# A two-layer graph attention kernel: VectorE ends layer 0's last chunk, x's product and layer 1's weights change place, and some steps change engine

## The reference

```python
# layer 0: x [4096,64], E [4096,64], adj [4096,4096] int32 (mostly 0)
scores = (x @ W @ a1)[:, None] + (E @ W @ a2)[None, :]
e = where(scores > 0, scores, 0.2 * scores); e = where(adj > 0, e, NEG_BIG)
x = layernorm(x + elu(softmax(e, axis=1) @ E + x))
# layer 1: the new x is on both sides
wh = x @ W1
e = leaky_relu((wh @ a_src)[:, None] + (wh @ a_dst)[None, :], 0.01)
x = layernorm(x + softmax(where(adj > 0, e, NEG_INF), axis=1) @ wh + bias)
```

## Time and profile before

| | |
|---|---|
| median of 3 runs | 646.89 us (645.05 to 647.01) |
| the profiled execution | 648.09 us, its span 646.3 us |
| busy: DVE, ACT, PE, POOL | 554.9, 535.4, 509.3, 178.7 us |
| granted PE clock, mean | 0.96 |
| DMA | 76.16 MB, most of it in the first half |

### The profile page before, as it was taken

One profiled execution on the slowest core, in us unless ns is written; L12 is line 12 of the kernel. 1 busy time (PEld: TensorE's weight loads), 2 busy tenths in 40 slices (PEclk: granted clock), 3 DMA queues, 4 the chain that ended last, 5 costly groups with the idle time before them and its releaser, 6 DMA issues.

```text
span 646.3 us, 14279 instructions
## 1 busy us (share of the span) xinstructions
PE 509.3 (79%) x6039; PEld 237.3 (37%) x6039; DVE 554.9 (86%) x758; ACT 535.4 (83%) x618; POOL 178.7 (28%) x116
## 2 busy tenths in 40 slices
PE   1307777889989799989987875578887988899994
PEld 1204444333443334434454532233333333333352
DVE  2899997999799998989669688877979998889795
ACT  0969993989999997899989687648997999689783
POOL 2241000266027830465001056005200340121050
PEclk9999787999999999999999898879999999989998
DMA  9998994766568636630100100000001000000000
GB/s 219 363 369 297 351 335 138 263 222 238 216 208 283 245 126 260 211 111 1 50 3 2 35 2 2 34 0 2 10 2 32 2 17 1 18 2 17 1 14 14
DMA packets 18252, 76.16 MB, mean 118 GB/s; under 512 B 6300, under 2 KB 8524, under 8 KB 9996
## 3 DMA queue, kind: packets, MB, share of 16 engines
q1 hardware_dynamic: 17304, 74.87, 33.0%
q0 software_dynamic: 112, 0.28, 0.2%
q10 hardware_dynamic: 772, 0.10, 0.1%
HBM read 74.16 MB, written 1.09 MB: 116 GB/s over the span
## 4 chain that ended last, share of the span: by engine, by line
issue 31%; DVE 25%; ACT 21%; PE 16%; POOL 5%; DMA 1%; ACTq 1%; POOLq 0%; DVEq 0%
ACT Pm L783 17%; DVE junk L903 11%; PE acc L1169 8%; DVE zps L1051 7%; PE zps L1224 5%; ACT zps L775 2%; DVE v L880 2%; PE acc L1176 1%; DMA acol<-in_L_gnn_weight_a 1%; POOL tAB L542 1%; POOL rstd L587 1%; DVE D L923 1%; POOL tAB L545 1%; DVE tot L965 0%; POOL o L526 0%
## 5 line engine op out<-in xcount | busy, mean ns | idle before, releaser
L783 ACT ACTIVATE Pm<-zps,ebias 128x1024 f32<-128x1024 f32 (+1 forms) x320 | 292.0, 934 | 60.3 <-DVE zps L1051 47.9
L1224 PE MATMUL zps<-D,v 128*128 128x128 bf16 x2048 | 166.8, 225 | 59.9 <-DVE D L923 32.6
L775 ACT ACTIVATE zps<-S_row,ntau_col 128x1024 f32<-128x1024 f32 (+1 forms) x203 | 195.1, 964 | 5.3
L1224 PEld LDWEIGHTS zps<-D,v 128*128 128x128 fp8e4 x2048 | 120.2, 100 | 201.5 <-ACT zps L775 89.6
L1169 PE MATMUL acc<-Pm,VE 128*32 128x512 f32 (+2 forms) x1280 | 148.8, 539 | 19.8 <-ACT Pm L783 13.7
L1051 DVE SCALAR_TENSOR_TENSOR zps<-S_row,tau_col,zps 128x1024 f32<-128x1024 f32 (+1 forms) x117 | 118.5, 1034 | 50.7 <-PE zps L1224 50.4
L1169 PE MATMUL acc<-Pm,X 128*32 128x512 f32 (+2 forms) x1280 | 141.8, 532 | 21.5 <-ACT Pm L783 20.1
L903 DVE CUSTOM_DVE_ANT_0 junk<-v,adj_in 128x2048 int8<-128x2048 int8 (+3 forms) x80 | 154.5, 1954 | 1.7 <-ACT adj_in L664 1.7
L903 DVE CUSTOM_DVE_ANT_0 junk<-v,u_row 128x2048 int8<-128x2048 int8 x64 | 152.4, 2397 | 0.2
L1176 PE MATMUL acc<-Pm,ones 128*32 128x256 f32 (+1 forms) x1280 | 87.8, 348 | 0.0
L518 POOL TENSOR_TENSOR tAB<-flag,totW 128x520 f32<-128x520 f32 (+1 forms) x8 | 10.9, 1366 | 260.3 <-issue 166.1
(11 more groups left out here) (163 smaller groups left out, 261.5 us busy)
## 6 DMA issues: line engine op xcount, KB each, us to landing
adj_in<-in_adj SPq DMA_DIRECT2D x62, 1024.0 KB, 5.5
S_row<-S_rows_scratch SPq DMA_DIRECT2D x6, 512.0 KB, 4.0
Pm<-in_adj SPq DMA_DIRECT2D x2, 1024.0 KB, 5.6
...
```

The lines of the kernel that those rows point to most:

```text
L775: a.activation(mask_of(n), S_row[:, C % 2, 0:R(C) * P], ACT.Relu, bias=ntau_col[:, layer(C), n % JT:n % JT + 1]).then_inc(seed_done, 1)
L783: a.activation(Pm_of(k, 0, R(C) * P), mask_of(k), ACT.Exp, bias=ebias[:, layer(C), int(seeded(k)), J:J + 1])\
L1224: last = t.matmul(mask[:, r * P:(r + 1) * P], v[:, chunks[C][1] + r, J * P:(J + 1) * P], D[:, C % 2, PART * second + r, :], start=(r * P % ...
```

## The change

It does five things.

1. `BY_VECTOR` takes in chunk 4, layer 0's last: its `add_up`, `normalise` and `scale` run on DVE within chunk 5, and POOL keeps the power. `IN_FIRST` moves these up (scores from step 19 to 13, the transposes of the rows from 22 to 18), `THIRD` lists the steps of the maxima over chunk 6's second stretch of columns, and the second `D` comes at step 22 and no longer at 25, with its weights apart (`weights_of_parts`, step 24).
2. x's product runs on DVE, just ahead of its sum, and no longer on POOL.
3. W0 goes first on SP's queue, ahead of E; a0, W1 and a1 stay on ACT's. The semaphore `w_loaded` is one for each layer, and the setup turns and spreads layer 0's weights alone. Layer 1's are repeated, turned and saved between chunk 0's row maxima, in PSUM of `acc`.
4. ACT does a Tanh on one column (`warm`) ahead of the first `convert`.
5. `SEEDS`: chunk 3 has 23 seeded steps and no longer 26, chunks 6 and 7 have 18 each and no longer 20.

```diff
-SEEDS = ((29, 28, 28, 26, 24), (20, 20, 20, 10, 0))
+SEEDS = ((29, 28, 28, 23, 24), (20, 18, 18, 10, 0))
-    IN_FIRST = dict(reciprocal=6, elu=8, sums=10, squares=14, scores=19, rows=22, maxima=23, second=25)
+    IN_FIRST = dict(add_up=5, elu=8, normalise=9, scores=13, rows=18, maxima=20, second=22, weights=24)
+    THIRD = (1, 3, 7, 11, 15, 16, 18, 23)
-    BY_VECTOR = (NC - 2, LAST)
+    BY_VECTOR = (NC - 2, NC - 1, LAST)
...
             if C == NC:
                 n = R(nxt)
-                return [(nxt, r, 1) for r in range(n) if 1 + r * 20 // n == J] + \
+                return [(nxt, r, 1) for r in range(n) if THIRD[r] == J] + \
                        [(NC, r, 3) for r in range(R(NC)) if at("maxima", C) + r // 2 == J] + \
-                       [(nxt, r, 2) for r in range(n) if at("second", C) + 1 + r * (JT - 3 - at("second", C)) // n == J]
+                       [(nxt, r, 2) for r in range(n) if at("weights", C) + r * 6 // n == J]
...
+            sp.dma_start(wraw[:, 0, :], W0).then_inc(w_loaded[0], 16)
             sp.dma_start(VE[:, :, :], E.rearrange("(n p) f -> p n f", p=P)).then_inc(e_loaded, 16)
...
-            pool.wait_ge(wbc_saved, 1)
-            pool.wait_ge(x_loaded, 16)
-            g.tensor_tensor(xprod, X[:, :, 0:F], wbc[:, 0, :].unsqueeze(1).broadcast_to([P, JT, F]), ALU.mult)\
-                .then_inc(xprod_done, 1)
...
+            a.activation(warm[:, :], tanh_bias[:, :], ACT.Tanh, bias=tanh_bias[:, :], scale=40.0)
             for H in range(SETUP_AT):
                 convert(H)
...
+            def repeat_weights(l):
+                dve.wait_ge(w_loaded[l], 48)
+                for k in range(2 * l, 2 * l + 2):
+                    d.tensor_copy(arep[:, k, :], acol[:, k:k + 1].broadcast_to([F, P])).then_inc(arep_done, 1)
...
-            dve.wait_ge(xprod_done, 1)
+            dve.wait_ge(x_loaded, 16)
+            link(d.tensor_tensor(xprod, X[:, :, 0:F], wbc[:, 0, :].unsqueeze(1).broadcast_to([P, JT, F]), ALU.mult))
             link(d.tensor_reduce(s_col[:, :], xprod, AX.X, ALU.add))
...
+                if n == 3:
+                    repeat_weights(1)
+                if n == 4:
+                    save_turned_W(1)
+                if n == 5:
+                    save_weights(1)
                 row_max(0, n // 2, n % 2)
...
+            def spread_weights(l):
+                pe.wait_ge(w_loaded[l], 48)
+                t.transpose(weights_at[l][0:F, 0:F], wraw[:, l, :], identf[0:F, 0:F]).then_inc(wT_turned, 1)
+                pe.wait_ge(arep_done, 2 * l + 2)
+                pe.wait_ge(wT_saved, l + 1)
+                for k in range(2 * l, 2 * l + 2):
+                    last = t.matmul(weights_at[l][:, (1 + k % 2) * F:(2 + k % 2) * F], arep[:, k, :], wT[:, l, :],
+                                    start=True, stop=True)
+                last.then_inc(wbc_done, 1)
```

More of the change, by code:

```diff
@@ L159, in build @@
         norm2, norm_inv, bound = (sb(n, [P, 2]) for n in ("norm2", "norm_inv", "bound"))
-        tanh_bias = sb("tanh_bias", [P, 1])
+        tanh_bias, warm = sb("tanh_bias", [P, 1]), sb("warm", [P, 1])
         acol = sb("acol", [F, 4])
@@ L193, in build @@
         acc = ctx.enter_context(nc.psum_tensor("acc", [P, 2, BANK], F32))
-        w_loaded, e_loaded, x_loaded = sem("w_loaded"), sem("e_loaded"), sem("x_loaded")
+        w_loaded = [sem("w_loaded0"), sem("w_loaded1")]
+        e_loaded, x_loaded = sem("e_loaded"), sem("x_loaded")
         adj_landed = [sem(f"adj_landed{b}") for b in range(AB + 1)]
@@ L628, in _ @@
             a = nc.scalar
[L629 to L633, removed]
+            for k in range(2):
+                act.dma_start(acol[:, k:k + 1], a0[k * F:(k + 1) * F, :]).then_inc(w_loaded[0], 16)
+            act.dma_start(wraw[:, 1, :], W1).then_inc(w_loaded[1], 16)
+            for k in range(2):
+                act.dma_start(acol[:, 2 + k:3 + k], a1[k * F:(k + 1) * F, :]).then_inc(w_loaded[1], 16)
             act.wait_ge(memsets, 1)
@@ L794, in _, with save_turned_W, save_weights @@
             d.memset(tanh_bias[:, :], -20.0).then_inc(bias_set, 1)
[L795 to L798, removed]
+            def repeat_weights(l):
+                dve.wait_ge(w_loaded[l], 48)
+                for k in range(2 * l, 2 * l + 2):
+                    d.tensor_copy(arep[:, k, :], acol[:, k:k + 1].broadcast_to([F, P])).then_inc(arep_done, 1)
+            def save_turned_W(l):
+                dve.wait_ge(wT_turned, l + 1)
+                d.tensor_copy(wT[:, l, :], weights_at[l][0:F, 0:F]).then_inc(wT_saved, 1)
+            def save_weights(l):
+                dve.wait_ge(wbc_done, l + 1)
+                d.tensor_copy(wbc[:, 2 * l:2 * l + 2, :], weights_at[l][:, F:3 * F]
+                              .rearrange("p (k f) -> p k f", f=F)).then_inc(wbc_saved, 1)
+            repeat_weights(0)
             dve.wait_ge(ident_done, 2)
@@ L803, in _ @@
             last.then_inc(pick_done, 1)
[L806 to L810 removed]
+            save_turned_W(0)
+            save_weights(0)
             dve.wait_ge(wbc_saved, 1)
@@ L864, in norms @@
             def norms():
+                dve.wait_ge(wbc_saved, 2)
                 link(d.tensor_tensor(wsq, wbc[:, 2:4, :], wbc[:, 2:4, :], ALU.mult))
@@ L946, in second_diagonals, with weights_of_parts @@
                 write_diagonals(NC, PART)
+            def weights_of_parts():
                 link(d.tensor_copy(g_parts[:, 1, :], g8[:, 0:PART]))
@@ L1057, in _ @@
                         second_diagonals()
+                    if C == NC and J == at("weights", C):
+                        weights_of_parts()
                     for piece in pieces_at(C, J):
@@ L1069, in _ @@
             t = nc.tensor
-            pe.wait_ge(w_loaded, 96)
-            pe.wait_ge(ident_done, 2)
-            for l in range(2):
-                last = t.transpose(zps[0:F, l, 0:F], wraw[:, l, :], identf[0:F, 0:F])
-            last.then_inc(wT_turned, 1)
-            pe.wait_ge(arep_done, 4)
-            pe.wait_ge(wT_saved, 1)
-            for k in range(4):
-                last = t.matmul(zps[:, 1, BANK + k * F:BANK + (k + 1) * F], arep[:, k, :], wT[:, k // 2, :],
-                                start=True, stop=True)
-            last.then_inc(wbc_done, 1)
+            def spread_weights(l):
[7 more added lines that the diff above has]
+                last.then_inc(wbc_done, 1)
+            pe.wait_ge(ident_done, 2)
+            spread_weights(0)
             def turn_rows(C):
@@ L1156, in product @@
                     if C == 0:
-                        pe.wait_ge(rows_saved, 1)
+                        pe.wait_ge(wbc_saved, 2)
                     else:
@@ L1200, in _ @@
             pe.wait_ge(u_saved, JT // GT)
+            pe.wait_ge(rows_saved, 1)
+            spread_weights(1)
             next_product = 0
```

8 lines of the change are left out of this document (2 added, 6 removed).

## The result

The changed kernel takes 651.42 us (median, 648.25 to 654.4), the kernel before beside it 645.73 (643.89 to 647.95). The ratio is 1.0082, 95% interval 1.0063 to 1.0101: slower by some 5.3 us, where 2.0 us faster was forecast. The profiled execution took 651.83 us, its span 650.0 (before 646.3).

A forecast was written before the change was run, and what follows sets the result against it. No engine bounds the whole, so it went by stretch: start −0.6, chunk 3 +1.1, chunk 5 −0.7, chunk 6 −1.2, chunk 7 −0.6, sum −2.0 us, from 646.89 to 644.8 after rounding; own range 643 to 647.2, chance 0.45.

The forecast's parts named there:

- Chunk 3: Three seeded steps moved from ScalarE to VectorE would cost +1.1 us, between +0.2 and +2.1.
- the price of step 24: Chunk 3: VectorE does step 24 late, its Exp comes 1.1 to 2.2 us late, ScalarE's next seed and TensorE's mask behind.
- step 10: Chunk 3: it falls into the 2.34 us VectorE idles ahead of the sums and costs nothing.
- take back part of the delay: Chunk 3: ScalarE's 3.4 us less to do recovers some of step 24's delay; half of the shortfall gives +0.2.
- Chunk 5: Waits gone −5.4, ten operations +4.5, a faster maximum −0.4, POOL's power wait +0.6: −0.7 us, between −1.3 and 0.
- the shared-port rule: Chunk 5: two-input VectorE and GpSimd operations fully block each other, making its gain larger; set aside for a maximum's 0.4 us.
- The start: Ahead of the first D: −0.6 us, from −1.0 (E's landing alone bounds) to +0.1; first row maximum at 24.0.
- the landing of a0: Setup: a loads take 5.6 to 6.6 us from issue, so a0 is there at 7.0 to 8.0.
- The figure of the Trainium skill: Setup: about 2.0 us per transfer besides bytes would land a0 at 3.4, leaving E the only bound; set aside.
- Chunks 6 and 7: Two seeds less each: −1.2 us in chunk 6 (−2.2 to 0), −0.6 in chunk 7 (−1.8 to +0.5).
- other rivals: Whole kernel: nothing is left, 646.6 us, chance 0.3; the small edits pay in full, 642 us, chance 0.14.
- The slower one: VectorE becomes the bound in chunks 3, 6, 7, four or more of seven moved steps uncovered: 650.3 us, chance 0.11.

The follow-up runs named there:

- third_later: Changed kernel with chunk 5's two 2048-column maxima of steps 15 and 16 moved behind step 17's SCALAR_TENSOR_TENSOR; ratio 1.0033 to the kernel before, chunk 5 at 52.52 us.
- best2: Changed kernel with chunk 3 at 26 seeds and chunk 5's two maxima moved behind step 17; ratio 0.9935 to the kernel before.
- start_10_18_18: Kernel before with the change's setup part, step 10 of chunk 3 unseeded, 18 seeds in chunks 6 and 7, chunk 5's old order; ratio 0.9955.

## Why the prediction was wrong

**Chunk 3 (+1.1, measured +4.3 in the profile, +5.6 by the ratios): the step that failed is the price of step 24.** The mechanism and the place were named (its Exp waiting for VectorE, TensorE's mask behind it), the size was not. Three parts: the Exp came 2.9 us late against the chunk's start and not 1.1 to 2.2, since step 10 was said to cost nothing in idle time and cost 0.7, by the maximum and POOL's products that then got into each other's way. Then TensorE lost the whole of it: the prediction let ScalarE's 3.4 us less of work "take back part of the delay", but that only brought ScalarE to the waiting Exp 1.65 us sooner against the chunk's start, and made its wait 4.52 us. And behind the pause TensorE ran 3.3 us at a granted clock of 0.54, 1.4 us of which the prediction had nothing. The range for the term ended at +2.1.

**Chunk 5 (−0.7, measured +2.4): the step that failed is the sum itself.** It added VectorE's waits and operations, which came out (the waits gone, ten operations of 0.42 to 0.43, no maximum above 2.29, 0.89 for the power), but VectorE is not what ends the chunk's steps; it never asked which SCALAR_TENSOR_TENSOR stands behind the moved work. The list of the third stretch's maxima put two of 2.28 us right ahead of step 17's. third_later shows it: the same sum of work with the two behind step 17 makes the chunk 3.05 us shorter. With that mended, a gain of the forecast's size is there: 0.7 us in the mean of the traces (0.8 at like clocks, 52.45 in best2 against 53.23 in start_10_18_18, both at 0.83), and 1.6 ± 1.4 by the ratios.

The prediction set the shared-port rule of the Trainium skill aside here, because a maximum lost only 0.4 us beside far longer pieces of POOL's. That reading was wrong, though the 0.4 itself was right. Rows of before around the maximum of 2.69 at 391.14:

```profile
386.85 0.68 POOL L543 TENSOR_TENSOR tAB<-tAB,X 128x256 f32<-128x256 f32 x1
...
389.03 2.66 POOL L549 TENSOR_TENSOR tAB<-tAB,mean 128x256 f32<-128x256 f32 x1 [0.74 <-DVE mean L966]
391.77 2.54 POOL L550 TENSOR_TENSOR tAB<-tAB 128x256 f32<-128x256 f32 x1
...
388.93 2.29 DVE L903 CUSTOM_DVE_ANT_0 junk<-v,adj_in 128x2048 int8<-128x2048 int8 x1
```

The piece of POOL's that was running when that maximum began had 0.55 us left, which bounds what VectorE could lose there. POOL lost the more: its pieces take 0.68 us while VectorE idles, and 2.3 to 2.7 where they began inside a maximum. So in this chunk the two did block each other, mostly at POOL's cost, and taking POOL's work away gave VectorE 0.4 us.

**The start (−0.6, measured −0.63)** was right in the end and partly by luck: the landing of a0 was taken from rows in which it was queued with E's bytes (5.6 to 6.6 us) and was 2.3 us in fact. The trace of before had the better row, that of W0, issued at 0.75 just ahead of E, with its size and the time from issue to landing:

```profile
o<-in_L_gnn_W ACTq DMA_DIRECT2D x1, 16.0 KB, 1.9
```

The figure of the Trainium skill, DMA: Bandwidth & Descriptors, that the prediction set aside there (some 2 us besides the bytes, given for the other queue) was the better one for loads ahead of E. E's landing, which the prediction named as the other bound, set the start all the same. With `warm` the table load stands at 6.01, out of the conversions' way; the kernel was not run without it.

**Chunks 6 and 7 (−1.8 together, −0.6 in the profiles, −2.1 ± 1.1 by the ratios)** were right in sign. Chunk 7 gives 0.12 us in every trace, less than the 0.6 forecast; that VectorE, busy 58.86 of 62.22, eats the rest is likely and not shown. Chunk 6 gives 0.4 to 0.7 at a granted clock of 0.92 and 1.3 at 0.97. VectorE's waits on masks from 25.4 us into chunk 6 fell from 4.4 to 1.4 us, where about 2 was forecast.

The prediction's sum and its other rivals add up as written. Its own range, −3.7 to +0.3, comes out at −3.9 to +0.2 when the five bounds are added as independent, which changes nothing.

**The rivals.** The slower one had the right place and nearly the right reason, VectorE late in chunk 3 and passed on in full, and its 650.3 is near the measured 651.42, but by other terms: it asked for chunks 6 and 7 as well, which took no harm, and it left out chunk 5, where the other half of the loss was. Its point, four or more of seven steps uncovered, was wrong in kind: one badly placed step in each chunk did it, in chunk 3 with two more that made VectorE late for it.
